# First self-attention: values and softmax denominators by one product, then brought into equal rows by transfers

## The reference

```python
qkv = (layernorm(x) @ W_qkv).reshape(8, 256, 3, 16, 16)        # 16 heads of 16
attn = einsum('bhqd,bhkd->bhqk', q, k) * 16 ** -0.5
attn = where(abs(i - j) <= 64, attn, -inf)                      # a band of 64 keys on each side
out = einsum('bhqk,bhkd->bhqd', softmax(attn), v)
x = x + out.reshape(8, 256, 256) @ W_proj + b_proj
```

## Time and profile before

| | us |
|---|---|
| median of 3 runs | 1519.23 (1513.35 to 1520.01) |
| the profiled execution | 1518.75 |
| its span | 1517.1 |
| TensorE busy in the span | 1436.5 (95%) |
| VectorE, ScalarE, GpSimd busy | 748.8, 618.9, 490.4 |
| the first self-attention, roughly | 20 to 225 of the span |

### The profile page before, as it was taken

How to read it: one execution, slowest core, us unless ns; L and a number is a source line. 1 busy time by engine, 2 the same in 40 slices (tenths; PEclk the granted TensorE clock), 3 DMA queues, 4 the chain that set the end, 5 groups by cost and what they waited for, 6 DMA issues and landing times. The chain is left out here.

```text
span 1517.1 us, 34544 instructions
## 1 busy us (share of the span) xinstructions
PE 1436.5 (95%) x11816; PEld 1158.5 (76%) x11817; DVE 748.8 (49%) x2160; ACT 618.9 (41%) x1711; POOL 490.4 (32%) x758
## 2 busy tenths in 40 slices
PE   7999978988999999999999999999799899999998
PEld 5676656666889999976777777776566578899997
DVE  6667746887533333344444444444278862222222
ACT  2433345654122212235445444545266533333332
POOL 3544441344421222123223223333124452222222
PEclk9999998999999999999999999999899999999999
DMA  9920000052233524220000000000001522533332
GB/s 316 333 62 2 2 2 8 30 174 69 57 91 86 150 52 129 34 63 1 1 1 1 1 1 1 1 1 0 1 16 44 172 78 39 148 92 93 92 90 34
DMA packets 79666, 97.46 MB, mean 64 GB/s; under 512 B 10523, under 2 KB 72579, under 8 KB 79555
## 3 DMA queue, kind: packets, MB, share of 16 engines
q1 hardware_dynamic: 64643, 77.58, 16.1%
q0 software_dynamic: 13680, 17.19, 6.5%
q10 hardware_dynamic: 1232, 1.18, 0.2%
HBM read 57.51 MB, written 39.59 MB: 64 GB/s over the span
## 5 line engine op out<-in xcount | busy, mean ns | idle before, releaser
L1717 POOL TENSOR_TENSOR L1a_prob<-L1a_prob,L1a_rtot 128x1024 f32<-128x1024 f32 x64 | 121.1, 1892 | 274.4 <-DVE L1a_rtot L1591 274.4
L2230 PEld LDWEIGHTS L0x_ps<-L0f_rows_t,L0f_w_up 128*128 128x128 f32 x1584 | 183.2, 193 | 10.9 <-issue 9.5
L2230 PE MATMUL L0x_ps<-L0f_rows_t,L0f_w_up 128*128 128x128 f32 x1584 | 185.4, 277 | 5.7 <-issue 4.8
L2306 ACT ACTIVATE L1f_hid<-L1x_ps,L1f_b_up 128x128 f32<-128x128 f32 x296 | 92.3, 363 | 164.4 <-PE L1x_ps L2230 161.6
L2230 PEld LDWEIGHTS L1x_ps<-L1f_rows_t,L1f_w_up 128*128 128x128 f32 x1184 | 140.2, 194 | 3.4 <-issue 1.6
L2230 PE MATMUL L1x_ps<-L1f_rows_t,L1f_w_up 128*128 128x128 f32 x1184 | 141.1, 278 | 0.6 <-ACT L1f_rows_t L2290 0.6
L2239 PE MATMUL L1x_ps<-L1f_w_down,L1f_hid 128*128 128x256 f32 x592 | 135.8, 383 | 1.9 <-DVE wv L2408 1.9
L2174 POOL TENSOR_TENSOR turn<-eps 128x1 f32<-128x1 f32 x74 | 13.6, 184 | 374.7 <-DVE wv L2408 371.1
L1659 ACT ACTIVATE L1a_prob<-L1a_ps_s,L1a_nmax 128x256 f32<-128x256 f32 x256 | 118.2, 473 | 38.1 <-DVE L1a_nmax L1586 38.1
L2239 PEld LDWEIGHTS L1x_ps<-L1f_w_down,L1f_hid 128*128 128x128 f32 x592 | 110.7, 192 | 16.0 <-issue 2.1
L1234 POOL TENSOR_SCALAR_AFFINE_SELECT L0a_prob<-L0a_prob 128x128 f32<-128x128 f32 (+1 forms) x256 | 79.7, 352 | 107.4 <-ACT L0a_prob L1189 107.4
(11 more groups left out here) (471 smaller groups left out, 2746.4 us busy)
## 6 DMA issues: line engine op xcount, KB each, us to landing
expert_table<-zero SPq DMA_DIRECT2D x1, 16640.0 KB, 68.4
L0f_w_up<-in_w_dram SPq DMA_DIRECT2D x8, 1408.0 KB, 6.9
L1f_w_up<-in_w_dram SPq DMA_DIRECT2D x8, 1024.0 KB
L1f_w_down<-in_w_dram SPq DMA_DIRECT2D x8, 1024.0 KB
L0f_w_down<-in_w_dram SPq DMA_DIRECT2D x8, 768.0 KB, 8.6
L1f_rows<-expert_table SPq DMA_DIRECT2D x35, 130.0 KB
L0f_rows<-expert_table SPq DMA_DIRECT2D x32, 130.0 KB
sums<-X SPq DMA_DIRECT2D x8, 256.0 KB
```

Source lines behind the costliest of these rows:

```text
L1717: eng.tensor_tensor(v, v, r.unsqueeze(2).to_broadcast([P, 2 * QT_N, S]), ALU.mult).then_inc(norm_done, 1)
L2230: ins = eng.matmul(ps_h[c][:, o:o + P], w_up[par][:, t, w0:w0 + P], rows_t[:, t, :], start=(t == 0), stop=(t == DT - 1))
L2306: ins = eng.activation(hid[:, c, k * P:(k + 1) * P], ps_h[c][:, k * P:(k + 1) * P], ACT.Gelu, bias=b_up[par][:, 2 * c + k:2 * c + k + 1])
```

## The change

The value weights of a head get the ones between the values: `v_s` is filled with 1.0 once, and ScalarE copies the values into every second column (even ones). A head's 32 weight columns are then value, one, value, one, ...; for an odd head the slice starts one column earlier, so that it is one, value, one, value. One set of products gives values in the even rows and denominators in the odd rows for v = 0, and the reverse for v = 1. The two units of a pair no longer share columns: v = 0 goes to columns 0 to 255 of `ps_o`, v = 1 to columns 256 to 511.

Values and their denominators are then in neighbouring rows. ScalarE copies the whole of `ps_o` to SBUF (`both`) at the start of an even unit, ahead of the exponentials, and issues four transfers from row to row within SBUF, each of 64 rows x 1 KB: two for the denominators (to `summed_t`) behind the second exponential, two for the values (to `valued_t`) behind the fourth. VectorE's reciprocal and multiplication read these two tiles. They move behind the four maxima of the unit, and so ahead of the taking out of keys. TensorE's next pair waits for the copy (`copied`), no longer for the multiplication (`o_out`).

The last two units (`direct`) keep two sets of products and read PSUM directly; for them the second half of the heads in the last batch's `v_s` is cleared to zero again by VectorE in unit 26, and the block of ones is laid out in alternate rows. The rows of `wo0` are put in the same alternating order on the host.

The diff, cut to its core:

```diff
@@ attention_banded, helpers
-        def odd_even(v):
-            return v.rearrange("p (a two) (half d) -> p a (two half) d", two=2, half=2)[:, :, 0::3, :]
+        def weights_of(i, t, head):
+            columns = v_s[i][:, t, :, :].rearrange("p h n -> p (h n)")
+            return columns[:, 2 * DH * head - head % 2:2 * DH * (head + 1) - head % 2]
+
+        def direct(u):
+            return u >= units - 2
@@ vector
-                    eng.memset(ones[:, v, v * DH:(v + 1) * DH], 1.0).then_inc(built, 1)
+                    eng.memset(ones[:, v, v::2], 1.0).then_inc(built, 1)
                 def sums(b, c):
-                    eng.wait_ge(values_done, 2 * (b * 2 + c + 1))
-                    eng.reciprocal(rsum[:, :], ps_o[:, S:2 * S]).then_inc(rsum_done, 1)
+                    n = b * 2 + c
+                    if n:
+                        eng.wait_ge(o_out, n)
+                    if direct(2 * n):
+                        eng.wait_ge(values_done, 2 * (n + 1))
+                        eng.reciprocal(rsum[:, :], ps_o[:, S:2 * S]).then_inc(rsum_done, 1)
+                    else:
+                        eng.wait_ge(sums_moved, 32 * (n + 1))
+                        eng.reciprocal(rsum[:, :], summed_t[:, :]).then_inc(rsum_done, 1)
                 def out(b, c):
...
-                    eng.tensor_tensor(o_t[:, c, :], ps_o[:, 0:S], rsum[:, :], ALU.mult).then_inc(o_out, 1)
+                    if not direct(2 * n):
+                        eng.wait_ge(values_moved, 32 * (n + 1))
+                    eng.tensor_tensor(o_t[:, c, :], ps_o[:, 0:S] if direct(2 * n) else valued_t[:, :], rsum[:, :], ALU.mult).then_inc(o_out, 1)
-                    eng.memset(v_s[i][:, :, :, :], 0.0).then_inc(cleared, 1)
+                    eng.memset(v_s[i][:, :, :, :], 1.0).then_inc(cleared, 1)
                     whole = part(u - 2)[:2] if v == 1 and u > 1 else None
-                    if whole:
-                        sums(*whole)
...
                     shift(u)
-                    if whole:
-                        out(*whole)
                     if u + 1 < units:
                         for r in range(GROUPS):
                             maximum(u + 1, r)
+                    if whole:
+                        sums(*whole)
+                        out(*whole)
+                    if u == units - 6:
+                        eng.wait_ge(values_done, u - 1)
+                        eng.memset(v_s[(B - 1) % 2][:, :, HEADS // 2:HEADS, :], 0.0).then_inc(cleared, 1)
                     for e in of(MID, u):
                         take(*e)
@@ scalar
+                def gather(n):
+                    eng.wait_ge(values_done, 2 * (n + 1))
...
+                    eng.activation(both[:, :, :], ps_o[:, :].rearrange("p (w s) -> p w s", w=2), ACT.Copy).then_inc(copied, 1)
+
+                def move(n, kind):
+                    eng.wait_ge(copied, n + 1)
+                    if n:
+                        eng.wait_ge(o_out, n)
+                    for w in range(2):
+                        if kind == "sums":
+                            eng.dma_start(summed_t[w::2, :], both[1 - w::2, w, :]).then_inc(sums_moved, 16)
+                        else:
+                            eng.dma_start(valued_t[w::2, :], both[w::2, w, :]).then_inc(values_moved, 16)
...
+                    pair = u // 2 - 1 if u % 2 == 0 and u else None
+                    if pair is not None:
+                        gather(pair)
                     for r in range(GROUPS):
                         exponential(u, r)
+                        if pair is not None and r % 2 == 1:
+                            move(pair, "sums" if r == 1 else "values")
@@ tensor, values(u)
-                            eng.wait_ge(o_out, u // 2)
-                    for summed in range(2):
+                            eng.wait_ge(copied, u // 2)
+                    for summed in range(2 if direct(u) else 1):
                         for t in range(KT):
                             for r in range(GROUPS):
-                                o = summed * S + first_key[t]
-                                lhs = ones[:, v, :] if summed else v_s[b % 2][:, t, c * 8 + 2 * r + v, :]
+                                o = (summed if direct(u) else v) * S + first_key[t]
+                                lhs = ones[:, v, :] if summed else weights_of(b % 2, t, c * 8 + 2 * r + v)
```

More of the change, by code:

```diff
@@ L996, in attention_banded @@
         rsum, o_t = sb("rsum", [P, S]), sb("o_t", [P, 2, S])
+        both, summed_t, valued_t = sb("both", [P, 2, S]), sb("summed", [P, S]), sb("valued", [P, S])
         built, cleared, tops_cleared = sem("built"), sem("cleared"), sem("tops_cleared")
@@ L1004, in attention_banded @@
         values_done, rsum_done, o_out = sem("values"), sem("rsum"), sem("o_out")
+        copied, sums_moved, values_moved = sem("copied"), sem("sums_moved"), sem("values_moved")
         projected, added, biased = sem("projected"), sem("added"), sem("biased")
@@ L1178, in take @@
                     else:
-                        eng.wait_ge(cleared, 2)
+                        eng.wait_ge(cleared, 3 if b == B - 1 else 2)
                         for t in range(KT):
-                            ins = eng.activation(odd_even(v_s[b % 2][:, t, :, :]), src[:, t, :].rearrange("p (a two d) -> p a two d", two=2, d=DH),
-                                                 ACT.Copy)
+                            ins = eng.activation(v_s[b % 2][:, t, :, 0::2], src[:, t, :].rearrange("p (h d) -> p h d", d=DH), ACT.Copy)
                     ins.then_inc(out_scalar, 1)
@@ L1190, in exponential @@
                                    ACT.Exp).then_inc(exp_done, 1)
+                def gather(n):
+                    eng.wait_ge(values_done, 2 * (n + 1))
+                    if n:
+                        eng.wait_ge(sums_moved, 32 * n)
+                        eng.wait_ge(values_moved, 32 * n)
+                    eng.activation(both[:, :, :], ps_o[:, :].rearrange("p (w s) -> p w s", w=2), ACT.Copy).then_inc(copied, 1)
+                def move(n, kind):
+                    eng.wait_ge(copied, n + 1)
+                    if n:
+                        eng.wait_ge(o_out, n)
[4 more added lines that the diff above has]
+                            eng.dma_start(valued_t[w::2, :], both[w::2, w, :]).then_inc(values_moved, 16)
                 for e in FIRST:
@@ L1330, in values @@
                         if u:
-                            eng.wait_ge(o_out, u // 2)
-                    for summed in range(2):
+                            eng.wait_ge(copied, u // 2)
+                    for summed in range(2 if direct(u) else 1):
                         for t in range(KT):
                             for r in range(GROUPS):
-                                o = summed * S + first_key[t]
-                                lhs = ones[:, v, :] if summed else v_s[b % 2][:, t, c * 8 + 2 * r + v, :]
-                                ins = eng.matmul(ps_o[rows(r), o:o + W], lhs, prob[u % 2][:, r, t, :], start=(v == 0 and not summed and t == 0),
-                                                 stop=(v == 1 and t == KT - 1), skip_group_check=True)
+                                o = (summed if direct(u) else v) * S + first_key[t]
+                                lhs = ones[:, v, :] if summed else weights_of(b % 2, t, c * 8 + 2 * r + v)
+                                ins = eng.matmul(ps_o[rows(r), o:o + W], lhs, prob[u % 2][:, r, t, :],
+                                                 start=(t == 0 and (v == 0 and not summed if direct(u) else True)),
+                                                 stop=(t == KT - 1 and (v == 1 or not direct(u))), skip_group_check=True)
                     ins.then_inc(values_done, 1)
@@ L2679, with in_turn @@
     down0[:, 0:full + GATED_TAIL] = i["L0_ffn_W3"].transpose(0, 2, 1)
+    def in_turn(w):
+        return w.reshape(-1, 2, 16, *w.shape[1:]).swapaxes(1, 2).reshape(w.shape)
     laid = {
@@ L2683 @@
         "wq0": qkv[:, 0:256], "wk0": qkv[:, 256:512], "wv0": qkv[:, 512:768],
-        "wo0": i["L0_attn_W_proj"], "bo0": i["L0_attn_b_proj"],
+        "wo0": in_turn(i["L0_attn_W_proj"]), "bo0": i["L0_attn_b_proj"],
         "wq1": i["L0_xattn_wq"].T, "wk1": i["L0_xattn_wk"].T, "wv1": i["L0_xattn_wv"].T, "wo1": i["L0_xattn_wo"].T,
```

3 lines of the change are left out of this document (2 added, 1 removed).

## The result

| | before | after |
|---|---|---|
| median, us | 1515.54 (7 runs, 1513.35 to 1520.01) | 1531.70 (7 runs, 1527.09 to 1537.77) |
| the profiled execution's span | 1517.1 | 1536.1 |

What follows compares the result with a forecast made beforehand. TensorE's product starts were taken to bound the first stage. Steps 1 to 4 summed to -3.3 us (1515.5); 42.5 for the fill's stop and 3 for the clock gave 1561; likeliest case 1554 to 1567, range down to 1511.

Steps and rivals of the forecast that it cites:

- Step 5: ScalarE's first transfer issue, unit 2, stands behind the expert table's fill: 42.5 us, plus 3 for the clock's return.
- the sign of the forecast: Whole kernel: slower, at a chance of 0.58; faster 0.11, no change that a measurement can tell 0.31.
- Step 1: TensorE, units 0 to 29: the second set of products, with ones, goes, saving 0.76 us each, 22.8 us.
- Step 2: Second units of batches 1 to 6: VectorE's later key copies delay TensorE's scores 2.0 us each, 12.0; batch 7 adds 1.0.
- slow landings: Rival: queues side by side, but transfers land late during the fill, 11 us: 1527, up to 1545; chance 0.10.
- Step 3: Value products wait for GpSimd's mask: 0.4 us at 7 batch borders, 2.9 us, and 0.6 in batch 0.
- Step 4: ScalarE's copies cost nothing; its 60 transfer issues cost 2 us in third units and 1.0 at the stage's end.
- Side by side: Rival: both queues served during the fill, landings in time: 1515.5, from 1512 to 1519; chance 0.30.
- The forecast's own cause: The fill's stop: the first issue on ScalarE's queue waits behind the fill, holding TensorE; 1561 us, chance 0.46.

Runs made afterwards that it cites:

- the fill later: Changed kernel with the expert table's fill issued only after unit 29's value products; one profiled execution, 1587 us for the whole, only the first stage compared.
- 3 idle products: Changed kernel plus 3 idle products on TensorE before the scores of units 7, 11, ..., 27; 1528.18 us, ratio 1.0021 to the kernel before.
- the keys first: Changed kernel with VectorE taking the keys out before the reciprocal and multiplication; 1508.06 us, ratio 0.9965 to the kernel before.
- the end filled: Version with the keys first plus 9 idle products before unit 31's scores and 9 before the last output projection; 1508.09 us, ratio 0.9966 to the kernel before.

## Why the prediction was wrong

**Step 5 failed**: the 42.5 us (and 3 for the clock behind them) that the first issue on ScalarE's queue was to stand, and with it the number. It measured 0.53 us. The forecast took the 56.08 us of SyncE's issue as a state of all hardware queues, because it was "the row of the same stretch". The runs show that ScalarE's queue is served beside it: issues of 0.47 to 0.63 us from 35.55 us on, and 65 us of standstill only when the same transfers are put on SyncE's queue. The row that argued against it stood in the forecast too: two issues at 0.84 us in 0.44 and 0.51 us. "Nearest" was measured by time and should have been measured by queue. The rule of the Trainium skill (Perfetto Trace Analysis, DMA Instruction, HWDGE), that a shared block is locked for exclusive use, gave 42 us here, and the measurement disagrees: ScalarE's two issues of 0.53 and 0.61 us lie inside SyncE's 56. The rule of the Trainium skill (DMA: Bandwidth & Descriptors, Queues, rings and completion order), that each DMA engine takes turns between queues, fits: issued in time, landing after 5.3 to 5.7 us instead of 1.8 to 1.9. That the sign of the forecast came out right is luck: without step 5 its sum is -3.3 us.

**Step 1, mis-sized.** I took the spacing of the second set, 0.76 us. But of two sets the first takes 0.67 us to the next start and the second 0.76, and a set that stands alone now takes 0.79 (99.83 to 100.62, and the same in later units), so 0.65 is saved, 19.5 us in all instead of 22.8. Why a last set takes longer no run shows. The sliced weights load in 109 ns, as before.

**Step 2, right in place and size**: 2.0 us forecast, 1.93 to 1.98 measured outside the fill, in batches 1 to 6. Its price was incomplete: the pause lowers the clock, 7.6 us in seven batches, a term that the forecast put at nothing. I had the clock in the forecast, for the long stop alone. In the fill the wait is 1.2 to 1.4 us longer, as the rival of slow landings had it for the second units.

**Step 3, right in place, somewhat less in all**: 0.4 us forecast at the border of batches, 0.42 measured at four, 0.24 at the two in the fill's stretch, none at the seventh, and 0.42 more than before in batch 0: 2.6 us instead of 3.5.

**Step 4, partly.** In the third units the turned scores still come 4.95 us after those of the unit before: no loss, because each issue begins while an exponential runs. ScalarE has the values out 4.3 us behind the turned scores (34.53 to 38.84) instead of 3.55, and 4.95 are there. The two places where the issues reach TensorE are unit 27 (0.8 us) and unit 31 (waits of 0.79, 0.69 and 0.48 us, 0.65 more than the 0.51 and 0.80 before; 1.0 forecast). At the end of the stage the low clock came on top: the scores of unit 31 and the last projections run at it, 3.9 of the 4.7 us.

**The rivals.** "Slow landings" came nearest in time (1527, which is 8 us over the execution that it starts from; 19 were measured). It holds for the fill, with 5.7 us instead of its 11: key waits 2.6 us longer, and 3.1 before the turned scores of units 4 and 8. The latter show that I had looked for the slack in the wrong place: a late landing in a fourth unit holds up VectorE's shift of the next unit. "Side by side" (-3.3 us) had the mechanism of the issues right and lacked the clock. From its -3.3 one comes to +13.3 by three measured terms: 7.6 for the clock, 5.7 for the landings, 3.3 that step 1 doesn't save. Most of the other 5.7 lie at the end of the stage, where the clock is low too, and behind it, where the profiled executions differ by more than that. The forecast's own cause accounts for none of it.

## What to carry to other kernels

When TensorE bounds a stage, price a new wait twice: by its length and by what the granted clock does behind it. Here the clock behind a pause of 1.9 to 3.4 us cost another 1.6 to 2.7 us where it fell, and idle products in the pause gave the 7.6 us of the clock back in seven batches. When work is moved later on one engine, list everything that is now queued behind it and follow each through the ring of buffers: swapping three VectorE calls turned 1.0098 into 0.9965. And price an issue from a row of the queue that will issue it.

## What the runs showed of the hardware

A pause of TensorE of 1.93 to 1.98 us lowered the granted clock in two of four cases of the changed kernel (the eight products of 116.11 us at full clock, those of 141.14 at the lower), in three of six without the transfers and in four of six with the fill later: nine of sixteen. Those of 2.3 us and more beside the fill lowered it each time (2.29 and 2.32, 3.17 and 3.39). But a pause of 2.85 us before the scores of unit 31 left it at 1.00 in the run with 3 idle products and lowered it with the keys first; one of 1.56 us lowered it in the run with the keys first and the end filled, while those of 1.55 us left it at 1.00 in the changed kernel and with the keys first. Pauses of 1.07 us lowered it in none of four. So a pause is what goes ahead of the fall, and its length alone doesn't decide; what else does stays open. A transfer of 64 KB between rows of SBUF landed in 1.8 to 1.9 us, and in 5.3 to 5.7 us (medians) beside a fill that kept the DMA engines busy (share 1.09), though it went by another queue. Issues on ScalarE's queue took 0.47 to 0.63 us and overlapped its running exponential.
